# Row norms of the updated inner weights in a fused AdaLN block: squares on ScalarE and sums on VectorE, one each per batch

## The reference

```python
w0 = _zeropower_ns5(dw0)            # five Newton-Schulz steps; w1, w2 alike
w0 = w0 + dw0
w0 = w0 / (norm(w0, axis=2) + 1e-05) * w0_norm      # a norm for every row
...
h = w2 @ qT
g = silu(w0 @ qT)
o = swapaxes(w1 @ (g * h), 1, 2)    # then RMS norm, output projection, residual,
                                    # layer norm, router, 16 experts (top 6), shared expert
```

## Time and profile before

| | us |
|---|---|
| three runs | 720.38, 719.37, 716.83 |
| median | 719.37 |
| span of the profiled execution | 715.6 |
| PE busy | 668.4 (93%) |
| DVE busy | 482.1 (67%) |
| ACT busy | 347.5 (49%) |
| POOL busy | 211.9 (30%) |

### The profile page before, as it was taken

How to read it: one execution, slowest core, us unless ns; L and a number is a source line. 1 busy time by engine, 2 the same in 40 slices (tenths; PEclk the granted TensorE clock), 3 DMA queues, 4 the chain that set the end, 5 groups by cost and what they waited for, 6 DMA issues and landing times.

```text
span 715.6 us, 11552 instructions
## 1 busy us (share of the span) xinstructions
PE 668.4 (93%) x4132; PEld 570.2 (80%) x4132; DVE 482.1 (67%) x958; ACT 347.5 (49%) x758; POOL 211.9 (30%) x210
## 2 busy tenths in 40 slices
PE   3989889779998799999999999999999999999997
PEld 2768779769997588877888888888888888888885
DVE  3787788959997378767545766566655666655555
ACT  2367669869998984573223232232322322323222
POOL 1345767954018665214200340012200321000000
PEclk9989999979999799999999999999999999999999
DMA  8000000011000000023002331224321332122223
...
DMA packets 20472, 41.48 MB, mean 58 GB/s; under 512 B 3360, under 2 KB 3616, under 8 KB 20288
## 3 DMA queue, kind: packets, MB, share of 16 engines
...
...
## 4 chain that ended last, share of the span: by engine, by line
PE 73%; ACT 9%; DVE 8%; POOL 3%; issue 3%; DMA 3%; ACTq 0%; DVEq 0%; POOLq 0%
PE ps L970 36%; PE ps L1041 18%; ACT junk L634 3%; PE ps L804 2%; PE ps L909 2%; PE ps L910 2%; PE ps L898 2%; PE ps L834 2%; PE ps L885 2%; DMA qkvw<-in_qkvw 2%; PE ps L921 1%; ACT junk L584 1%; PE ps L988 1%; PE ps L1007 1%; DVE sq L1155 1%
## 5 line engine op out<-in xcount | busy, mean ns | idle before, releaser
L705 ACT ACTIVATE sgm<-ps,zero 128x512 f32<-128x512 f32 x100 | 68.9, 690 | 273.1 <-PE ps L970 273.1
L970 PE MATMUL ps<-h2hi,whi 128*128 128x512 f32 x400 | 156.1, 390 | 0.0
L970 PE MATMUL ps<-h2lo,whi 128*128 128x512 f32 x400 | 155.7, 389 | 0.0
L970 PE MATMUL ps<-h2hi,wlo 128*128 128x512 f32 x400 | 155.6, 389 | 0.0
L1446 DVE TENSOR_TENSOR am<-sgm,ps 128x512 f32<-128x512 f32 x88 | 60.5, 688 | 136.9 <-ACT sgm L705 136.8
L447 POOL CAST whi<-raw 128x768 fp32r<-128x768 f32 x25 | 22.0, 879 | 237.1 <-DMA raw<-in_moew 235.8
L970 PEld LDWEIGHTS ps<-h2lo,whi 128*128 128x128 f32 x400 | 75.1, 188 | 15.6
L970 PEld LDWEIGHTS ps<-h2hi,whi 128*128 128x128 f32 x400 | 75.1, 188 | 15.6
L970 PEld LDWEIGHTS ps<-h2hi,wlo 128*128 128x128 f32 x400 | 75.1, 188 | 15.4
L1041 PE MATMUL ps<-ahi,whi 128*128 128x512 f32 x200 | 77.9, 390 | 0.1
L1041 PE MATMUL ps<-ahi,wlo 128*128 128x512 f32 x200 | 77.8, 389 | 0.0
...
## 6 DMA issues: line engine op xcount, KB each, us to landing
...
```

What stands on the lines that cost most here:

```text
L705: ac.activation(sgm[:, n % 2, :], gate_bank(n), ACT.Silu, bias=zero[:, :]).then_inc(S["e_sg"], 1)
L970: last = mm(o, w_, a_[:, kc, tok], start=(kc == 0 and k == 0), stop=(kc == KC - 1 and k == 2))
```

## The change

The six squares with accumulation of a batch become one square of 128x768 on ACT (into a new tile `wsq`, two buffers) and one reduction on DVE. The root stays on POOL. The sum with 1e-5, the reciprocal (now an instruction of its own) and the product with the old norm move to DVE, each waiting for the one before. The first square is put two group steps ahead of the end of Newton-Schulz, its reduction and its scales into DVE's Newton-Schulz loop, its root between the POOL sums of groups 9 and 10. The first `gate_hidden` on PE comes ahead of the last two turned groups. The other scales of DVE stand behind `oss`, in front of `gh`.

```diff
--- before.py
+++ after.py
@@ -168,6 +168,7 @@
...
             ("ahi", [P, 4, BLK], F32R), ("alo", [P, 3, BLK], F32R), ("cw", [P, 3, BLK], F32)])
         assert end <= R_tmp + 20480
+        wsq = [at("wsq0", [P, 6, P], F32, R_tmp + 16384), at("wsq1", [P, 6, P], F32, R_q + 12288)]
         (raw,), end = carve(R_tmp + 20480, [("raw", [P, 2, WCOLS], F32)])
         assert end <= R_wo
...
@@ -452,32 +453,27 @@
...
                 split_weights(j)
 
+            def row_roots(b):
+
+                m = slice(6 * b, 6 * b + 6)
+                po.wait_ge(S["rss_ok"], b + 1)
+                po.tensor_tensor(rowsn[:, m], rows[:, m], half[:, 0:6], ALU.pow).then_inc(S["ws_pow"], 1)
+
             for g in range(NGRP):
+                if g == NGRP - 2:
+                    row_roots(0)
                 po.wait_ge(S["x_sb"], NGRP * (NS_STEPS - 1) + g + 1)
                 wv = dw[:, g * MPG:(g + 1) * MPG, :]
                 po.tensor_tensor(wv, wv, X[:, g * MPG:(g + 1) * MPG, :], ALU.add).then_inc(S["w_ok"], 1)
 
-            def row_scales(b):
-
-                m = slice(6 * b, 6 * b + 6)
-                po.wait_ge(S["rss_ok"], 6 * (b + 1))
-                po.tensor_tensor(rowsn[:, m], rows[:, m], half[:, 0:6], ALU.pow).then_inc(S["ws_chain"], 1)
-                po.wait_ge(S["ws_chain"], 3 * b + 1)
-                po.tensor_scalar(rowsi[:, m], rowsn[:, m], L2_EPS, None, ALU.add).then_inc(S["ws_chain"], 1)
-                po.wait_ge(S["ws_chain"], 3 * b + 2)
-                po.tensor_tensor(rowsn[:, m], rowsi[:, m], mone[:, :], ALU.pow).then_inc(S["ws_chain"], 1)
-                po.wait_ge(S["ws_chain"], 3 * b + 3)
-                po.tensor_tensor(wsc[:, b, :], rowsn[:, m], wnorm[:, :], ALU.mult).then_inc(S["w_scale"], 1)
-
-            po.wait_ge(S["wn_ok"], 1)
-            for b in range(3):
-                row_scales(b)
+            for b in (1, 2):
+                row_roots(b)
             for b in range(B):
 
...
                 po.tensor_tensor(rr[:, 4 * b:4 * b + 4], oss[:, 4 * b:4 * b + 4], mhalf[:, :], ALU.pow).then_inc(S["rr_ok"], 1)
                 if b + 3 < B:
-                    row_scales(b + 3)
+                    row_roots(b + 3)
 
                 t = TPB * b
@@ -610,6 +606,13 @@
...
             for g in (6, 8):
                 first_turned(g)
+            def row_squares(b):
+
+                ac.wait_ge(S["w_ok"], (6 * b + 5) // MPG + 1)
+                if b >= 2:
+                    ac.wait_ge(S["rss_ok"], b - 1)
+                ac.activation(wsq[b % 2][:, :, :], dw[:, 6 * b:6 * b + 6, :], ACT.Square, bias=zero[:, :]).then_inc(S["wsq_ok"], 1)
+
             for r in range(NGRP * NS_STEPS + 2):
                 n = r
@@ -625,13 +628,9 @@
...
                     ac.activation(X[:, g * MPG:(g + 1) * MPG, :], bank(4 + n % 2).rearrange("p (a d) -> p a d", d=P),
                                   ACT.Copy).then_inc(S["x_sb"], 1)
-            def row_squares(b):
-
-                ac.wait_ge(S["w_ok"], (6 * b + 5) // MPG + 1)
-                for m in range(6 * b, 6 * b + 6):
-                    if m:
-                        ac.wait_ge(S["rss_ok"], m)
-                    ac.activation(junk[:, :], dw[:, m, :], ACT.Square, bias=zero[:, :], accum_out=rows[:, m:m + 1]).then_inc(S["rss_ok"], 1)
+                if r == NGRP * NS_STEPS - 2:
+                    row_squares(0)
+            row_squares(1)
 
             def exponentials(half):
@@ -654,10 +653,9 @@
...
                                   scale=wsc[:, b, 3 * h:3 * h + 1], bias=zero[:, :]).then_inc(S["g_ok"], 1)
 
-            for b in range(2):
-                row_squares(b)
+            row_squares(2)
             gate_out(0)
-            for b in range(2, 4):
+            for b in (3, 4):
                 row_squares(b)
             for s in range(B + 1):
@@ -683,10 +681,10 @@
...
                                       scale=modc[:, CB, c, b:b + 1], bias=modc[:, SB_, c, b:b + 1]).then_inc(S["h2_ok"], 1)
                     ac.wait_ge(S["h2_ok"], KC * (b + 1))
-                    ac.wait_ge(S["rss_ok"], min(NMAT, 6 * (b + 6)))
+                    ac.wait_ge(S["wsq_ok"], min(B, b + 6))
                     ac.activation(h2hi[:, :, tok], h2T[:, :, tok], ACT.Copy).then_inc(S["hi_ok"], 1)
-                for b in {0: (4, 5), 1: (6,), 2: (7,)}.get(s, ()):
-                    row_squares(b)
+                if s + 5 < B:
+                    row_squares(s + 5)
 
             def high(n):
@@ -870,6 +868,18 @@
...
             frob_sums(B - 1)
             NR = NGRP * NS_STEPS
+
+            def weights_turned(g):
+
+                pe_.wait_ge(S["w_ok"], g + 1)
+                if g >= 2:
+                    pe_.wait_ge(S["wt_sb"], g - 1)
+                else:
+                    pe_.wait_ge(S["t_sb"], NR - NGRP)
+                for a in range(MPG):
+                    last = pe_.transpose(bank(6 + g % 2)[:, a * P:(a + 1) * P], dw[:, g * MPG + a, :], ident[:, :])
+                last.then_inc(S["wt_ps"], 1)
+
             for r in range(NR + 4):
                 n = r
@@ -921,24 +931,16 @@
...
                     last.then_inc(S["t_ps"], 1)
                 n = r - 4
-                if n >= NR - NGRP:
-                    g = n % NGRP
-                    pe_.wait_ge(S["w_ok"], g + 1)
-                    if g >= 2:
-                        pe_.wait_ge(S["wt_sb"], g - 1)
-                    else:
-                        pe_.wait_ge(S["t_sb"], NR - NGRP)
-                    for a in range(MPG):
-                        last = pe_.transpose(bank(6 + g % 2)[:, a * P:(a + 1) * P], dw[:, g * MPG + a, :], ident[:, :])
-                    last.then_inc(S["wt_ps"], 1)
-
-
-            pe_.wait_ge(S["x_sb"], NR)
-            pe_.wait_ge(S["wt_sb"], NGRP)
+                if NR - NGRP <= n < NR - 2:
+                    weights_turned(n % NGRP)
+
             def gate_hidden(b):
 
                 if b >= 1:
                     pe_.wait_ge(S["gh_ok"], NH * b)
+                else:
+                    pe_.wait_ge(S["b_sb"], NR)
+                    pe_.wait_ge(S["wt_sb"], 2)
                 for h in range(NH):
                     for o, j in ((bank(2), 0), (bank(3), 2)):
@@ -971,6 +973,10 @@
...
 
             gate_hidden(0)
+            for g in range(NGRP - 2, NGRP):
+                weights_turned(g)
+            pe_.wait_ge(S["x_sb"], NR)
+            pe_.wait_ge(S["wt_sb"], NGRP)
             outputs(0)
             for s in range(B + 2):
@@ -1268,6 +1274,28 @@
...
             x_init(B - 1)
             NR = NGRP * NS_STEPS
+            n_w = 0
+
+            def wstep(ins):
+                nonlocal n_w
+                n_w += 1
+                ins.then_inc(S["ws_chain"], 1)
+                ve.wait_ge(S["ws_chain"], n_w)
+
+            def row_sums(b):
+
+                ve.wait_ge(S["wsq_ok"], b + 1)
+                ve.tensor_reduce(rows[:, 6 * b:6 * b + 6], wsq[b % 2][:, :, :], AX.X, ALU.add).then_inc(S["rss_ok"], 1)
+
+            def row_scales(b):
+
+                m = slice(6 * b, 6 * b + 6)
+                ve.wait_ge(S["ws_pow"], b + 1)
+                wstep(ve.tensor_scalar(rowsi[:, m], rowsn[:, m], L2_EPS, None, ALU.add))
+                wstep(ve.reciprocal(rowsn[:, m], rowsi[:, m]))
+                ve.wait_ge(S["wn_ok"], 1)
+                ve.tensor_tensor(wsc[:, b, :], rowsn[:, m], wnorm[:, :], ALU.mult).then_inc(S["w_scale"], 1)
+
             for r in range(NR + 5):
                 if r in (1, 3):
@@ -1289,6 +1317,10 @@
...
                     ve.wait_ge(S["wt_ps"], g + 1)
                     ve.tensor_copy(WT[:, g * MPG:(g + 1) * MPG, :], bank(6 + g % 2).rearrange("p (a d) -> p a d", d=P)).then_inc(S["wt_sb"], 1)
+                if r == NR:
+                    row_sums(0)
+                if r == NR + 2:
+                    row_scales(0)
 
             n_r = 0
@@ -1356,7 +1388,11 @@
...
                                             in1=g_sb[:, b % 2, h, :], op0=ALU.mult, op1=ALU.mult).then_inc(S["gh_ok"], 1)
 
+            row_sums(1)
+            row_sums(2)
             gate_hidden(0)
+            row_sums(3)
+            row_sums(4)
             for s in range(B + 1):
                 b = s
@@ -1383,6 +1419,7 @@
...
                     ve.tensor_scalar(oss[:, cols], bank(7)[:, cols], 1.0 / HD, LN_EPS, ALU.mult, ALU.add).then_inc(S["oss_v"], 1)
                 if s + 1 < B:
+                    row_scales(s + 1)
                     gate_hidden(s + 1)
                 if s >= 2:
@@ -1402,6 +1439,8 @@
...
                     ve.wait_ge(S["agg2"], TPB * (b + 1))
                     ve.tensor_scalar(var2[:, b * TPB:(b + 1) * TPB], mv[:, b * TPB:(b + 1) * TPB, 1], LN_EPS, None, ALU.add).then_inc(S["var2"], 1)
+                if s + 5 < B:
+                    row_sums(s + 5)
 
             def low(n):
```

2 lines of the change are left out of this document (1 added, 1 removed).

## The result

The changed kernel takes 722.39 us (median of nine runs, 720.39 to 725.53), the kernel before takes 718.72 us beside it (nine runs, 715.12 to 721.26). The ratio formed from all the runs is 1.0064, with a 95% interval of 1.0042 to 1.0086: slower, by 3.0 to 6.2 us. The two medians alone would give 1.0051. The forecast was a ratio of 1.0075.

What follows compares the result with a forecast made beforehand. The prediction took the output stage's chain of waits (ACT, PE, DVE), then PE in the experts, as the bound. A 1.9 us lead less the losses in output steps 0 to 6 gave -5.4, so 724.8 us, range 721.0 to 727.0.

Steps and rivals of the forecast that it cites:

- head: Stretch before the first output step, DVE and PE idle until the first gate; claimed a lead of 1.9 us at its oss.
- step 0: First of eight output steps, one per batch; claimed 0.05 us lost to scales, 0.88 to a sum, 0.64 regained on ACT.
- step 1: Second output step; claimed 0.39 us lost to scales, 0.88 to a sum of row squares, 0.20 regained on ACT.
- step 2: Third output step; claimed 0.98 us lost to scales, 0.88 to a sum of row squares, 0.20 regained on ACT.
- steps 3 to 5: Steady output steps, 7.29 us from osq to osq before; claimed 0.98 us longer each, 2.94 us in all.
- step 6: Output step whose x updates ran without a wait; claimed a 1.3 us loss, passed on to the experts.
- The scales: Output stage: scales behind oss delay ACT's gate, so gh starts 1.32 us later and each steady step grows 0.98 us.
- The sums: Three reductions on DVE between statistics and oT, ending the first three output steps; claimed 0.88 us each, 2.64 us in all.
- PE keeps its clock: Rival before the first output step: shorter PE idling keeps 2.4 GHz, lead 3.75 us instead of 1.9, 722.9 us; chance 0.13.
- A cheap gate: Rival: gh does not wait for the gate, so an output step costs only 0.34 us; 721.1 us, chance 0.08.
- The steps hide it all: Rival: PE lateness of 1.0 us or more ahead of the second x update hides scales and gate; 719.1 us, chance 0.07.
- The ports: Rival: DVE's scale multiplication waits for POOL's power, 0.7 us later in each of seven steps; 729.9 us, chance 0.07.

Runs made afterwards that it cites:

- e1: Changed kernel with the next batch's scales on DVE moved ahead of the wait for the oss sums; 717.57 us, ratio 0.9992 to the kernel before.
- e3: e1 plus three small DVE instructions of the same kind on unread scratch data at the old place behind oss; 719.13 us, ratio 1.0013.
- e12: Changed kernel with four unread products added on PE ahead of its wait for osq in output steps 1 to 3; 723.06 us, ratio 1.0057.
- e2: Changed kernel with row-square sums 5 to 7 moved ahead of the next output step's wait for oss, scales left behind oss; 719.37 us, ratio 1.0012.
- e4: Changed kernel with the edits of e1 and e2 together; 713.24 us, ratio 0.992 to the kernel before.
- e5: e4 with POOL's root of batch 0 between weight sums 10 and 11 instead of 9 and 10; 711.67 us, ratio 0.9908.

## Why the prediction was right, and where its terms were not

In terms of the forecast (us, a gain is positive; the head counts from the last X copy to oss(0), step 0 from there to osq(1)):

| | head | step 0 | step 1 | step 2 | steps 3 to 5 | step 6 | sum |
|---|---|---|---|---|---|---|---|
| forecast | 1.9 | -0.29 | -1.07 | -1.66 | -2.94 | -1.3 | -5.4 |
| profile after | 3.56 | -0.24 | -2.30 | -2.21 | -3.00 | -1.39 | -5.6 |

**The scales** were right in mechanism and size: 1.0 us a step (0.98 forecast), and e1 takes exactly that away. Its split was off. The forecast valued the DVE time alone at 0.34 us (0.59 less the wait of 0.25). e3 shows 0.16: the three instructions push gh back by 0.50 us, since they overlap by some hundredths, and of that 0.35 is taken up between gh and the statistics (3.31 us in e1, with PE's wait, 2.96 in e3). The same slack is in the sum for the whole: 1.34 less 0.35 is 0.99. So "a sixth" is what the DVE time costs alone; whatever is added first uses up the slack, and the gate's 0.84 us without the DVE time would by the same sum cost 0.49, which no run shows.

**The sums** were right in place, and with them the sizes: 0.94 us for a reduction (0.95 forecast), 0.93 for a square. A sum on the circle costs 0.82 us (e12 beside e2; 0.88 forecast), and with the clock held (e12) steps 1 and 2 are within 0.06 us of the forecast. The 0.20 us that ACT was to give back in each of them is there as well: 7.28 and 7.29 us in e4, for 7.49 before.

**The head** was mis-sized: 3.5 us, not 1.9. The first gh came 0.74 us earlier than I put it (233.16 for 233.9): I let the first square push the last Br on DVE back by 0.6, and it stands at 224.26, beside 224.20 before. Half of the difference is a smaller push: from the Br ahead of it to the last one are 1.51 us, for 1.21 before, so the push is 0.30. The rest is that the Newton-Schulz groups stood 0.24 us earlier in this execution. So the reduction, the root at 226.49 and all behind them come some 0.6 us earlier than I put them. The push of 0.30 us falls on the last X copy too (7.80 us behind the sixth X copy ahead of it, for 7.50 before). It lies ahead of the point from which I count, and is a cost that the two tables don't hold. gate_hidden(1) took 2.81 us and not 3.39, as the clock came back within it. That step of the working failed: I took its length from the kernel before, and it depends on when the clock falls and returns. Before, the clock fell in 233 to 235, here at 231. The length is luck in part: in e1, e4 and e2, with the same instructions ahead of it, it was 2.97, 2.96 and 3.62 us.

**What I missed** are the falls in steps 1 and 2. The sums on the circle make PE wait 1.09 and 1.08 us for osq there, and the forecast priced that as a plain delay. It cost 1.8 us more than that in the profile. The kernel before showed that such a thing happens, in its step 0, behind a wait of 1.05 us; I read that product only as slow. So the net loss of 5.6 us beside a forecast of 5.4 rests in part on two misses that cancel: 1.7 us more of a lead, 1.8 us more of a loss. That the sum came out so near is luck; the term for the steady steps is not.

**The rivals.** That PE keeps its clock in the head: no, 0.51 in 231 to 233. A cheap gate: no (e3). The steps hide it all: no, the slack among the x updates is 0.35 us, not 1.0. The ports: not in the steps. There the last of the scales ran at 240.14 in its usual 0.17 us, in the middle of POOL's power of 128x4 (239.88, 1.01 us). But in the head the scales were held up: the addition at 227.88 took 1.12 us instead of 0.16 and the multiplication at 229.25 took 0.85 instead of 0.17, and they end at 229.00 and 230.10, where POOL's two weight sums end (227.81 and half of 2.27, and 230.08). The reciprocal between them, which reads one tensor, ran beside the second sum in 0.19 us. In e5, with one weight sum behind the root, only the addition is held up (1.12), and the multiplication has its 0.17 again. The Trainium skill (SBUF — State Buffer, "Who interferes with whom") gives such a rule, an exclusive use of a pair of ports that DVE shares with GpSimd, for instructions with two SBUF inputs and for tensor_scalar in its two-port modes; that the addition ran in such a mode no run shows. Beside POOL's sums of 128x512 the trace agrees with it, beside its small powers it doesn't.

A sum of the prediction is off: 0.7 us in each of seven steps on top of 724.8 is 729.7, not the 729.9 that it gives for this rival; nothing hangs on it.

The marks named in the prediction stood as it has them: gh 1.4 us behind oss with an idle time that g_sb ended, g_sb by the scales, 8.3 us from osq to osq in steps 3 to 5. For step 2 it has 9.1 and the profile 9.70. The measured difference is 3.7 us between the medians and 5.3 between the spans. The ratio's interval (3.0 to 6.2 us) holds both; the last tenths are not resolved.

Open is how often the clock falls at each of these places. In the profile of e1 the products were slow in step 1 (3.02 us) and not in step 2 (1.89), though PE had waited 1.09 and 1.08 us for osq ahead of them. In that of e3 they were slow in both (3.43 and 2.85), in those of e2 and e4, with waits under 0.3 us, in neither. One profile of a kernel doesn't tell how its other executions went.
